# Softmax sums of a 32-head attention inverted by log and exp on ScalarE, with its matrix bursts moved to every fourth place

## The reference

```
def _L1_attn_ref(x, w_qkv, w_out, b_out, ln_gamma, ln_beta):      # HEADS = 32, DIM_HEAD = 32
    q, k, v = x @ w_qkv, by heads
    dots = q @ k.T * DIM_HEAD ** -0.5
    attn = softmax(dots, axis=-1)
    out = (attn @ v, heads side by side) @ w_out + b_out
    return layernorm(out) * ln_gamma + ln_beta
x = x + _L1_attn_ref(_layernorm(x), ...)
```

## Time and profile before

| | |
|---|---|
| median of 3 runs | 2024.59 us (2024.28 to 2027.73) |
| profiled execution, its own time | 2025.36 us |
| its span | 2023.6 us |
| PE busy | 1781.0 us (88%) |
| DVE busy | 1626.9 us (80%) |
| ACT busy | 1291.7 us (64%) |
| POOL busy | 1135.7 us (56%) |
| first and last transpose of the maxima (L1106) | 1064.8 and 1956.0 us |

### The profile page before, as it was taken

The page is one execution under the profiler, slowest core; times in us unless marked ns, Lnnn a source line. Parts: engine busy times, 40 slices in busy tenths (PEclk is TensorE's granted clock), DMA queues, the critical chain, the costliest instruction groups (busy, mean ns, idle before and its releaser), DMA issues. The chain is left out here.

```text
span 2023.6 us, 49215 instructions
## 1 busy us (share of the span) xinstructions
PE 1781.0 (88%) x18950; PEld 823.9 (41%) x18950; DVE 1626.9 (80%) x3052; ACT 1291.7 (64%) x2719; POOL 1135.7 (56%) x712
## 2 busy tenths in 40 slices
PE   6538857999999955968999999999999999999997
PEld 3337832233333344654433344434444343444334
DVE  7942567999999475438778999999999999999963
ACT  5403243888888710217866677777877777777785
POOL 8723541000000055331136888999999999989995
PEclk9768976899999956989998999999999999999998
DMA  1220045111111061137993323323232323233211
GB/s 48 36 50 3 1 147 191 42 48 42 46 48 39 13 201 52 48 96 265 386 386 87 83 67 82 80 69 82 68 85 64 85 66 83 72 77 77 73 28 42
DMA packets 194493, 180.22 MB, mean 89 GB/s; under 512 B 58740, under 2 KB 155124, under 8 KB 194052
## 3 DMA queue, kind: packets, MB, share of 16 engines
q1 hardware_dynamic: 185860, 170.01, 28.9%
q0 software_dynamic: 2944, 7.10, 1.1%
q10 hardware_dynamic: 5504, 0.73, 0.2%
HBM read 101.16 MB, written 75.26 MB: 87 GB/s over the span
## 5 line engine op out<-in xcount | busy, mean ns | idle before, releaser
L977 DVE TENSOR_REDUCE maxima_l<-max_l 128x1 f32<-128x512 f32 x1024 | 652.0, 678 | 46.5 <-PE max_l L1087 40.2
L953 POOL TENSOR_TENSOR part_sums_l<-probs_l 128x1024 f32<-128x1024 f32 x256 | 615.2, 2403 | 98.2 <-ACT probs_l L1043 85.4
L1043 ACT ACTIVATE probs_l<-exp_l 128x512 f32<-128x512 f32 x1024 | 568.1, 598 | 139.5 <-PE exp_l L1098 135.2
L1087 PE MATMUL max_l<-k_stack_l,q_stack_l 96*128 96x512 f16 x1024 | 399.3, 391 | 4.2 <-DVE pv_bank_l L969 3.3
L1098 PE MATMUL exp_l<-q_stack_l,k_stack_l 100*128 100x512 f16 x1024 | 389.6, 381 | 2.5 <-ACT probs_l L1043 1.6
L1305 DVE TENSOR_REDUCE maxima_l<-max_l 128x1 f32<-128x512 f32 x512 | 317.0, 682 | 17.0 <-PE max_l L1391 16.8
L1342 ACT ACTIVATE probs_l<-exp_l 128x512 f32<-128x512 f32 x512 | 279.3, 599 | 58.5 <-PE exp_l L1404 54.8
L1132 PE MATMUL pv_bank_l<-probs_l,v_ring_l 128*32 128x512 f32 x2048 | 273.6, 606 | 0.3 <-issue 0.3
L1819 POOL IOTA rows_e<- 128x32 int32 x1 | 0.2, 184 | 386.5 <-POOLq L26 386.5
L1087 PEld LDWEIGHTS max_l<-k_stack_l,q_stack_l 96*128 96x128 f16 x1024 | 100.0, 98 | 280.7 <-DVE maxima_l L977 189.8
L984 DVE TENSOR_TENSOR part_sums_l<-part_sums_l 128x512 f32<-128x512 f32 x128 | 182.3, 1424 | 14.4 <-POOL part_sums_l L953 14.3
(11 more groups left out here) (297 smaller groups left out, 2563.1 us busy)
## 6 DMA issues: line engine op xcount, KB each, us to landing
scratch_qk_l<-parts_g SPq DMA_DIRECT2D x128, 256.0 KB, 9.2
q_stack_l<-scratch_qk_l SPq DMA_DIRECT2D x192, 128.0 KB
k_stack_l<-scratch_qk_l SPq DMA_DIRECT2D x192, 128.0 KB
scratch_v_l<-v_g SPq DMA_DIRECT2D x16, 1024.0 KB
v_ring_l<-scratch_v_l SPq DMA_DIRECT2D x64, 256.0 KB, 3.3
scratch_stack_l<-parts_c SPq DMA_DIRECT2D x16, 384.0 KB, 3.6
q_stack_l<-scratch_stack_l SPq DMA_DIRECT2D x64, 96.0 KB, 2.2
k_stack_l<-scratch_stack_l SPq DMA_DIRECT2D x64, 96.0 KB, 2.3
```

The lines of the kernel that those rows point to most:

```text
L953: pool.tensor_tensor(part_sums[:, i, h, :, :], probs[:, i, h, 0:2, :], probs[:, i, h, 2:4, :], ALU.add).then_inc(pair_sum.sem, 1)
L977: dve.reduce_max(maxima[:, s % 2, at % NT, at // NT:at // NT + 1], max_bank(n, at)[:, :], AX).then_inc(max_taken.sem, 1)
L1043: act.activation(probs[:, i, at // NT, at % NT, :], exp_ps[at % 2][:, :], ACT.Exp, scale=a.scale).then_inc(prob_tile.sem, 1)
L1087: pe.matmul(max_bank(n, at)[:, :], qs[0:SHIFT_ROW, s % RING, h, k * P:(k + 1) * P], ks[0:SHIFT_ROW, s % RING, h, :], start=True, stop=True ...
```

## The change

The sums stay in the layout in which they are made. ACT takes their logarithm out of `sums_bank` at place 12 and the exp of its negative at place 14, which gives the inverses in `inv_rows`; the copies, the eight transposes and the reciprocal go. The values are no longer copied: DVE reads `pv_bank` itself when it normalises. The half sums of heads 2 and 3 are made by a tensor_reduce over a rearranged view of both halves, into a tile of its own, `key_sums`. The bursts stand at places 2, 6, 10, 14, the sums behind the third, and burst j waits for the last probability tile with its own key tile (12 + j). The other constants move as the diff shows. A table set with log and exp is loaded by name on entry.

```
-MAXT_AT, SHIFT_AT = 2, 4
-VALUES_AT, VALUES_COPY_AT = (1, 4, 7, 11), 11
-HALVES_ADD_AT = (2, 4)
-SUMS_AT, SUMS_COPY_AT, SUMST_AT = 7, 7, (9, 9)
-INVERSE_AT, INVERSE_ROWS_AT, INVERSET_AT, NORMALISE_AT = 9, 11, (13, 15), 0
-OUT_AT = (3, 5, 13, 15)
+MAXT_AT, SHIFT_AT = 1, 6
+VALUES_AT = (2, 6, 10, 14)
+HALVES_ADD_AT = (2, 6)
+SUMS_AT, LOG_AT, INVERSE_AT, NORMALISE_AT = 10, 12, 14, 0
+OUT_AT = (4, 8, 12, 15)
...
+BESIDE_ACT = ({(0, at): ("sum", 0, k) for k, at in enumerate((2, 5, 8, 11))}
+              | {(1, at): ("square", 0, k) for k, at in enumerate((2, 5, 8, 11))}
+              | {(3, 5): ("shift", 0, 0), (3, 8): ("normal", 0, 0), (3, 11): ("normal", 0, 1), (4, 2): ("normal", 0, 2), (4, 5): ("normal", 0, 3)}
+              | {(6, at): ("sum", 1, k) for k, at in enumerate((2, 5, 8, 11))}
+              | {(7, at): ("square", 1, k) for k, at in enumerate((2, 5, 8, 11))}
               | {(10, 5): ("shift", 1, 0)})
...
-                        dve.tensor_tensor(both[:, 0, :], both[:, 0, :], both[:, 1, :], ALU.add).then_inc(key_sum2.sem, 1)
-                    if at == INVERSE_AT and exists(turn, s, PV_LAG):
...
-                        dve.reciprocal(inv_sums[:, :, :], by_token[:, :, :, 0]).then_inc(inv_ready.sem, 1)
+                        dve.tensor_reduce(key_sums[:, HALVES_ADD_AT.index(at), :], both.rearrange("p a t -> p t a"), AX, ALU.add).then_inc(key_sum2.sem, 1)
                     if at == NORMALISE_AT and exists(turn, s, OUT_LAG):
-                        dve.wait_ge(inv_ps.sem, inv_ps.made(n - OUT_LAG, 0))
-                        dve.wait_ge(pv_sb.sem, pv_sb.made(n - OUT_LAG, 0))
-                        dve.tensor_tensor(oT[:, s % 2, :], oT_raw[:, :], sums_bank[:, :], ALU.mult).then_inc(oT_ready.sem, 1)
+                        dve.wait_ge(inv_ready.sem, inv_ready.made(n - OUT_LAG, 0))
+                        dve.wait_ge(pv_ps.sem, pv_ps.made(n - OUT_LAG, 0))
+                        dve.tensor_tensor(oT[:, s % 2, :], pv_bank[:, :], inv_rows[:, :], ALU.mult).then_inc(oT_ready.sem, 1)
...
+            act.preload_act_table_set("natural_log_exp_and_others")
...
-                        act.copy(sums[:, :], sums_bank[:, :]).then_inc(sums_sb.sem, 1)
...
-                        act.copy(inv_rows[:, :, :, :], bc(inv_sums[:, :, :], HEAD_ROWS)).then_inc(inv_rows_ready.sem, 1)
...
+                            act.wait_ge(inv_ready.sem, inv_ready.made(n - OUT_LAG, 0))
+                        act.activation(log_sums[:, :], sums_bank[:, :], ACT.Ln).then_inc(log_ready.sem, 1)
+                    if at == INVERSE_AT and exists(turn, s, PV_LAG):
+                        act.wait_ge(log_ready.sem, log_ready.made(n - PV_LAG, 0))
...
-                        act.copy(oT_raw[:, :], pv_bank[:, :]).then_inc(pv_sb.sem, 1)
+                        act.activation(inv_rows[:, :], log_sums[:, :], ACT.Exp, scale=-1.0).then_inc(inv_ready.sem, 1)
...
-                            pe.wait_ge(oT_ready.sem, oT_ready.made(n - OUT_LAG, 0))
+                            pe.wait_ge(log_ready.sem, log_ready.made(n - OUT_LAG, 0))
                         pe.transpose(sums_bank[0:TILES, 0:P], maxima[:, (s - 1) % 2, :, :], g.ident[:, :]).then_inc(maxT_ps.sem, 1)
...
+                        pe.wait_ge(prob_tile.sem, prob_tile.made(m, TILES - NT + j))
                         if j == 0:
                             pe.wait_ge(v_loaded[slot], nth(turn, s - PV_LAG, 16))
-                            pe.wait_ge(prob_tile.sem, prob_tile.made(m, TILES - 1))
...
-                                pe.wait_ge(pv_sb.sem, pv_sb.made(m - 1, 0))
+                                pe.wait_ge(oT_ready.sem, oT_ready.made(m - 1, 0))
...
+                            ins = pe.matmul(sums_bank[hh * HEAD_ROWS:(hh + 1) * HEAD_ROWS, :], ones[:, :],
+                                            part_sums[:, i, hh, 0, :] if hh < HG // 2 else key_sums[:, hh - HG // 2, :],
```

More of the change, by code:

```diff
@@ L854, in attention @@
         part_sums = sb("part_sums", [P, 2, HG, 2, N])
+        key_sums = sb("key_sums", [P, HG // 2, N])
         ones = sb("ones", [P, HEAD_ROWS])
@@ L857, in attention @@
         shift = sb("shift", [TILES, 2, P], F16)
-        sums, oT_raw, oT = sb("sums", [P, N]), sb("oT_raw", [P, N]), sb("oT", [P, 2, N])
-        inv_sums, inv_rows = sb("inv_sums", [P, NT, HG]), sb("inv_rows", [P, NT, HG, HEAD_ROWS])
+        log_sums, inv_rows, oT = sb("log_sums", [P, N]), sb("inv_rows", [P, N]), sb("oT", [P, 2, N])
         cleared = sem("cleared")
@@ L870, in attention @@
         pair_sum, key_sum, key_sum2 = made("pair_sum", HG), made("key_sum", HG // 2), made("key_sum2", HG // 2)
-        sums_ps, sums_sb, sumsT_ps = made("sums_ps"), made("sums_sb"), made("sumsT_ps")
-        inv_ready, inv_rows_ready, inv_ps = made("inv_ready"), made("inv_rows_ready"), made("inv_ps")
-        pv_ps, pv_sb, oT_ready, y_ps, y_taken = made("pv_ps"), made("pv_sb"), made("oT_ready"), made("y_ps"), made("y_taken")
+        sums_ps, log_ready, inv_ready = made("sums_ps"), made("log_ready"), made("inv_ready")
+        pv_ps, oT_ready, y_ps, y_taken = made("pv_ps"), made("oT_ready"), made("y_ps"), made("y_taken")
         def exists(turn, s, lag):
@@ L983, in step @@
                         both = part_sums[:, (s - PV_LAG) % 2, h, :, :]
-                        dve.tensor_tensor(both[:, 0, :], both[:, 0, :], both[:, 1, :], ALU.add).then_inc(key_sum2.sem, 1)
-                    if at == INVERSE_AT and exists(turn, s, PV_LAG):
-                        dve.wait_ge(sumsT_ps.sem, sumsT_ps.made(n - PV_LAG, 0))
-                        by_token = sums_bank[:, :].rearrange("p (k h r) -> p k h r", k=NT, h=HG)
-                        dve.reciprocal(inv_sums[:, :, :], by_token[:, :, :, 0]).then_inc(inv_ready.sem, 1)
+                        dve.tensor_reduce(key_sums[:, HALVES_ADD_AT.index(at), :], both.rearrange("p a t -> p t a"), AX, ALU.add).then_inc(key_sum2.sem, 1)
                     if at == NORMALISE_AT and exists(turn, s, OUT_LAG):
-                        dve.wait_ge(inv_ps.sem, inv_ps.made(n - OUT_LAG, 0))
-                        dve.wait_ge(pv_sb.sem, pv_sb.made(n - OUT_LAG, 0))
-                        dve.tensor_tensor(oT[:, s % 2, :], oT_raw[:, :], sums_bank[:, :], ALU.mult).then_inc(oT_ready.sem, 1)
+                        dve.wait_ge(inv_ready.sem, inv_ready.made(n - OUT_LAG, 0))
+                        dve.wait_ge(pv_ps.sem, pv_ps.made(n - OUT_LAG, 0))
+                        dve.tensor_tensor(oT[:, s % 2, :], pv_bank[:, :], inv_rows[:, :], ALU.mult).then_inc(oT_ready.sem, 1)
                     if at == TILES - 1 and s == OUT_LAG - 1 and exists(turn, s, OUT_LAG):
@@ L1044, in step @@
                                        scale=a.scale).then_inc(prob_tile.sem, 1)
-                    if at == SUMS_COPY_AT and exists(turn, s, PV_LAG):
+                    if at == LOG_AT and exists(turn, s, PV_LAG):
                         act.wait_ge(sums_ps.sem, sums_ps.made(n - PV_LAG, 0))
-                        act.copy(sums[:, :], sums_bank[:, :]).then_inc(sums_sb.sem, 1)
-                    if at == INVERSE_ROWS_AT and exists(turn, s, PV_LAG):
-                        act.wait_ge(inv_ready.sem, inv_ready.made(n - PV_LAG, 0))
                         if exists(turn, s, OUT_LAG):
-                            act.wait_ge(inv_ps.sem, inv_ps.made(n - OUT_LAG, 0))
-                        act.copy(inv_rows[:, :, :, :], bc(inv_sums[:, :, :], HEAD_ROWS)).then_inc(inv_rows_ready.sem, 1)
-                    if at == VALUES_COPY_AT and exists(turn, s, PV_LAG):
-                        act.wait_ge(pv_ps.sem, pv_ps.made(n - PV_LAG, 0))
+                            act.wait_ge(inv_ready.sem, inv_ready.made(n - OUT_LAG, 0))
+                        act.activation(log_sums[:, :], sums_bank[:, :], ACT.Ln).then_inc(log_ready.sem, 1)
+                    if at == INVERSE_AT and exists(turn, s, PV_LAG):
+                        act.wait_ge(log_ready.sem, log_ready.made(n - PV_LAG, 0))
                         if exists(turn, s, OUT_LAG):
                             act.wait_ge(oT_ready.sem, oT_ready.made(n - OUT_LAG, 0))
-                        act.copy(oT_raw[:, :], pv_bank[:, :]).then_inc(pv_sb.sem, 1)
+                        act.activation(inv_rows[:, :], log_sums[:, :], ACT.Exp, scale=-1.0).then_inc(inv_ready.sem, 1)
                     if at == SHIFT_AT and exists(turn, s, 1):
@@ L1143, in step @@
                         for hh in range(HG):
-                            ins = pe.matmul(sums_bank[hh * HEAD_ROWS:(hh + 1) * HEAD_ROWS, :], ones[:, :], part_sums[:, i, hh, 0, :],
+                            ins = pe.matmul(sums_bank[hh * HEAD_ROWS:(hh + 1) * HEAD_ROWS, :], ones[:, :],
+                                            part_sums[:, i, hh, 0, :] if hh < HG // 2 else key_sums[:, hh - HG // 2, :],
                                             start=True, stop=True)
                         ins.then_inc(sums_ps.sem, 1)
[L1147 to L1163, removed]
             for n in range(M + OUT_LAG):
```

## The result

The changed kernel is slower: 2047.22 us median of 5 (2040.68 to 2050.9) against 2024.62, which is the median of 5 runs of the kernel before; the ratio is 1.0101 (95% interval 1.008 to 1.0122). The forecast was 2044, slower.

The account below looks back on a forecast made before the run. PE bounds a plain step and never waits in the kernel before. 60 steps of 14.39 us, plus 12.4 and 3.8, less 856.0, give +23.6; tail -4; so 2024.59 + 19.6 = 2044 us, range 2016 to 2088.

Parts of the forecast that it names:

- the walk: One plain step followed by distances between starts, from exp product 14 to the next: 14.39 us, against 14.12 before.
- The price of the reduction: Each new half-sum reduction of 1,024 SBUF elements on DVE takes 1.22 us, from rows of shorter reductions.
- Rival A: New reduction is slow, 1.9 us, from its alternating source or POOL beside it: 82 us more, 2126 us; chance 14%.
- Stall 3: Max product 10 on PE waits for DVE behind the second new reduction: 0.48 us a step.
- Stall 2: Max product 6 on PE waits for DVE behind the first new reduction: 0.43 us a step.
- Stall 1: Value burst 2 on PE waits for normalise to finish reading the bank it overwrites: 0.25 us a step.
- Norm work at place 11: ACT's norm work between tiles 11 and 12 delays exp product 14 by 0.32 or 0.41 us; 12.4 us in all.
- The y add: DVE's add at place 15, in 7 steps, moves the chain by 0.54 us each: 3.8 us in all.
- Tail: Behind the last group, shorter work from sums to normalise, and the two steps before losing some transposes: -4 us.
- rival C: ACT's table sets are swapped each step, two loads of 1.28 us: +120 us, 2164 us; chance 3%.
- Rival B: Coupling is softer than walked and PE keeps its order, 13.24 us a step: 1972 us; chance 11%.
- turning point: Stalls smaller by 0.33 us a step, so a new reduction of 1.06 us or less.

Follow-up runs that it names:

- experiment 9: Changed kernel with half-sum reductions behind tiles 4 and 7, first value burst at place 3, norm work at 3, 6, 9, 12: 1977.63 us.
- experiment 1: Changed kernel with its two half-sum reductions on DVE behind tiles 4 and 7 instead of 2 and 6: 2003.32 us.
- experiment 2: Changed kernel with ACT's norm work at places 1, 4, 7, 10 instead of 2, 5, 8, 11: 2033.89 us.
- experiment 6: Changed kernel with the old wait, the first value burst waiting for all 16 probability tiles: 2044.64 us.
- experiment 5: Kernel before with only the half sums of heads 2 and 3 made by the reduction instead of the add, at the old places: 2018.32 us.
- experiment 8: Changed kernel's arithmetic in the old order of places, with ACT's copy of the values at place 11 kept and read by normalise: 2062.63 us.
- experiments 4: Changed kernel with the half sums made by the old add of two SBUF operands instead of the reduction: 2052.79 us.

## Why the prediction was right

Direction, size and mechanism came out: PE, the engine that bounds, lost more in waits than the 0.88 us that left it, at the three places that the walk names, twice behind DVE's new reductions and once behind normalise. Two of its terms were off by about 0.1 us a step in opposite directions, which the chain hides.

- **What bounds.** The distances between PE's starts held. They sum to 13.24 for the work that is left; experiment 9, without the three stalls, takes 13.45. Some of the 0.2 between them lies in exp products 2 and 3, which start 0.08 and 0.04 late; the rest was not traced.
- **The price of the reduction**, 1.22, was measured at 1.22 with POOL at work beside it. Rival A falls: neither the alternating read nor POOL adds anything to the 1.22 that the rows of shorter plain reductions led to. On the read the Trainium skill (Vector Engine (DVE) Microarchitecture Reference, The SBUF access granule: adjacent pairs) agrees in its exception: it states that a one-source stream alternating between two regions measured at the full read rate.
- **A misreading.** The prediction took the 1.14 that it worked out from the Trainium skill for the reduction's duration, and said that the sum would be 10 us lower by it. The walk already held the chain for 1.14 only, and the trace has 1.14 from the start of the new reduction to the start of the next (1194.91 to 1196.05), beside a duration of 1.22. The Trainium skill (Vector Engine (DVE) Microarchitecture Reference, Rate slope and fixed cost) gives its 75 ns an instruction after queue overlap, measured over instructions back to back. So 1024 columns at 1.04 ns and 75 ns make 1.14, an estimate, for the distance from start to start; the trace agrees, and nothing comes off the sum.
- **Stalls 2 and 3**: max 6 and max 10 start within 0.01 us of the walk (table), and experiment 1 shows the reductions' places as the cause: moved, the waits are gone. Stall 3, 0.48, measured 0.45. Stall 2, 0.43, measured 0.30, because stall 1 in front of it was longer and max 6 waits for DVE either way.
- **Stall 1**, 0.25, measured 0.35 (3.83 instead of 3.48): PE takes 0.14, not the 0.05 of the prediction, to start the burst behind normalise. The 0.05 was read from a weight load. That the step still came out at 14.39 is luck of this order: max 6, held by DVE either way, takes up what stall 1 adds.
- **Norm work at place 11**, 0.32 for sums and 0.41 for squares and normals, measured 0.29 (14.68) and 0.38 (14.77): 11.3 us in all instead of 12.4. Experiment 2 takes all of it away.
- **The y add**, 0.54, measured 0.54 (15.22 against 14.68; 14.93 against 14.39 in experiment 2).
- **Tail** -4, measured -3.7 in this pair of executions; experiment 6, which differs from the changed kernel by one wait, has a tail of 62.7 against 63.9, so the tenths mean little. From log to normalise it is 2.56 us, where the old way took 5.67: 3.1 gone instead of the 3.5 forecast.
- **Log and exp** take 0.60 and 0.66 (priced at 0.59 each), and both hide under burst 14. One table load stands on entry and none in the steps, so rival C did not occur. Rival B did not either: the reduction stayed above its turning point of 1.06, and PE waited where the walk has it wait.
- **Not foreseen:** waiting adds had held PE in one early step and in some norm steps of the kernel before (experiment 5), while the prediction has PE never wait there in a plain step. These waits make some 5 us of the 856 from which the sum starts; as the 856 were measured, the sum does not suffer.

## What to carry to other kernels

When an engine is the bound and a small ring ties it to a second one that is nearly as busy, a change that takes work from the first can still lengthen the step, if its new order makes the first wait. What counts is how far the two run apart between places, against the depth of the ring. Here it paid to put the second engine's long instructions one or two places behind the first's bursts (experiment 1), and the first burst one place further behind the work that it waits for (experiment 9). Walk one step with distances between starts before moving anything. An operand moved from one memory to another can change how long an instruction takes, by what another engine does at the time (experiment 8), so check what that engine is doing.

## What the runs showed that was not expected

- An instruction of DVE with two SBUF operands takes 0.68 us at its shortest and up to 2.9 beside POOL's 2.36 us sums (experiments 4 and 8), and the sums themselves are drawn out up to 2.91. Normalise with one operand in PSUM takes 0.68 to 0.69, and the reduction of one SBUF operand 1.22 to 1.25, in all of their records in the changed kernel.
- The same program can lock in different phases: in experiment 8 plain steps of 15.31 follow each other until the first norm work, and later plain steps come at 13.89. Why the long phase is stable was not tried.
